# Turning a group's row maxima with VectorE's 32x32 transpose and eight small transfers instead of a TensorE transpose

## What is computed

```python
q = x @ q_w.T + q_b
xd = conv(x, stride 2) + conv_b
k = xd @ k_w.T + k_b
v = xd @ v_w.T + v_b
att = jnp.einsum('bhnd,bhmd->bhnm', q, k) * scale
att = jax.nn.softmax(att, axis=-1)
out = jnp.einsum('bhnm,bhmd->bhnd', att, v)
return out @ out_w.T + out_b
```

## Time and profile before

| | us |
|---|---|
| median of 3 runs | 3911.18 |
| lowest and highest run | 3905.49, 3913.1 |
| span of the profiled execution | 3912.8 |
| TensorE busy | 3836.0 (98%) |
| VectorE busy | 3334.3 (85%) |
| ScalarE busy | 2612.8 (67%) |

### The profile page before, as it was taken

The page is one execution under the profiler, slowest core; times in us unless marked ns, Lnnn a source line. Parts: engine busy times, 40 slices in busy tenths (PEclk is TensorE's granted clock), DMA queues, the critical chain, the costliest instruction groups (busy, mean ns, idle before and its releaser), DMA issues. The chain is left out here.

```text
span 3912.8 us, 76603 instructions
## 1 busy us (share of the span) xinstructions
PE 3836.0 (98%) x22744; PEld 1996.5 (51%) x22744; DVE 3334.3 (85%) x4142; ACT 2612.8 (67%) x4969; POOL 844.9 (22%) x553
## 2 busy tenths in 40 slices
PE   8979999999999999999999999999999999999998
PEld 5643333333333333333333333333334899999998
DVE  9979998999899899989989998999996777777775
ACT  4428887888788788878878887888887334343343
POOL 6522100000000000000000000000001787787775
PEclk9979999999999999999999999999999999999999
DMA  8991133115103311510231051024111222222220
GB/s 295 345 201 58 50 48 56 33 34 70 34 27 49 56 33 34 70 34 27 47 57 34 29 68 38 30 46 59 33 36 58 78 85 83 67 86 78 72 86 27
DMA packets 315388, 269.34 MB, mean 69 GB/s; under 512 B 156593, under 2 KB 225201, under 8 KB 315314
## 3 DMA queue, kind: packets, MB, share of 16 engines
q1 hardware_dynamic: 314194, 264.36, 27.6%
q0 software_dynamic: 1120, 4.19, 0.4%
HBM read 157.30 MB, written 110.10 MB: 68 GB/s over the span
## 5 line engine op out<-in xcount | busy, mean ns | idle before, releaser
L751 DVE TENSOR_REDUCE half_max<-first_ps 128x2 f32<-128x1024 f32 x2038 | 2402.0, 1221 | 280.1 <-PE first_ps L590 276.1
L717 ACT ACTIVATE probs<-score_ps 128x512 f32<-128x512 f32 x4096 | 2114.7, 603 | 578.4 <-PE score_ps L615 577.8
L615 PE MATMUL score_ps<-q_s,k_s 49*128 49x512 f32 x4096 | 1444.2, 477 | 23.5 <-DMA q_s<-max_row 12.8
L615 PEld LDWEIGHTS score_ps<-q_s,k_s 49*128 49x128 f32 x4096 | 574.6, 185 | 1284.4 <-ACT probs L717 1156.1
L625 PE MATMUL pv_ps<-probs,v_s 128*32 128x512 f32 x8192 | 1102.2, 610 | 0.0
L590 PE MATMUL first_ps<-k_s,q_s 48*128 48x512 f32 x4076 | 903.3, 421 | 14.2 <-PEq L189 9.5
L860 POOL TENSOR_TENSOR num<-num,rden 128x1024 f32<-128x1024 f32 x2 | 4.7, 2373 | 2585.3 <-DMA rden<-rden_d 2585.3
L1035 ACT ACTIVATE act_f<-fc_ps,b 128x512 f32<-128x512 f32 x256 | 174.9, 684 | 470.4 <-PE fc_ps L988 468.3
L590 PEld LDWEIGHTS first_ps<-k_s,q_s 48*128 48x128 f32 x4076 | 408.6, 188 | 61.5 <-issue 10.9
L1112 DVE CAST a_hi<-act_f 128x512 fp32r<-128x512 f32 x256 | 241.9, 946 | 146.6 <-ACT act_f L1035 146.0
L1164 POOL TENSOR_TENSOR a_lo<-act_f,a_hi 128x512 fp32r<-128x512 f32 x256 | 339.4, 1331 | 86.1 <-DVE a_hi L1112 86.1
(11 more groups left out here) (109 smaller groups left out, 2540.0 us busy)
## 6 DMA issues: line engine op xcount, KB each, us to landing
q_s<-q_hi_d SPq DMA_DIRECT2D x512, 64.0 KB, 2.1
o_d<-o_sb SPq DMA_DIRECT2D x128, 256.0 KB, 2.1
x_t<-x_c_in SPq DMA_DIRECT2D x32, 512.0 KB, 5.8
q_hi_d<-q_hi SPq DMA_DIRECT2D x32, 512.0 KB, 4.8
q_lo_d<-q_lo SPq DMA_DIRECT2D x32, 512.0 KB, 5.1
k_s<-k_hi_d SPq DMA_DIRECT2D x128, 128.0 KB, 4.3
q_s<-q_lo_d SPq DMA_DIRECT2D x256, 64.0 KB, 2.1
x_res<-x_in SPq DMA_DIRECT2D x32, 512.0 KB
```

Of the source, the lines that this page charges most:

```text
L615: pe.matmul(bank(s, u)[:, :], k_s[g][at, a, t * P:(t + 1) * P], q_s[g][at, a, :], start=True, stop=True).then_inc(scored, 1)
L717: nc.scalar.activation(probs[s % 2][:, u, :], bank(s, u)[:, :], ACT.Exp).then_inc(exped, 1)
L751: dve.reduce_max(half_max[g % 2][:, :, a * TT + t, keys], first_ps[keys][:, :, :], AX.X)\
```

## The change

The maxima are no longer turned by TensorE. `neg_max` becomes 128 x 32 (16 columns used, the others set to zero once) and VectorE transposes it in four 32x32 squares: in square k, the partitions 32k to 32k+15 then hold the 16 rows for the queries 32k to 32k+31. `max_row` therefore has the 16 rows in four pieces on four groups of partitions, and SP assembles the row of q_s with eight transfers in place of two: two halves of the heads x four squares, each from 8 partitions with 128 bytes of each. TensorE's `turn_max` and its two waits are gone, and so is the turn's slot in the ring of score banks; since 4 x 32 scores per block don't divide by 3, one bank is skipped at each block's first step, with the waits adapted. VectorE's `rows` keeps its place in the order and waits for `maxed` instead of `turned`.

```diff
-        neg_max = [sb(f"neg_max{i}", [P, TT * HG]) for i in two]
-        max_row = [sb(f"max_row{i}", [TT * HG, P], F32R) for i in two]
+        SQ = 32
+        neg_max = [sb(f"neg_max{i}", [P, SQ], F32R) for i in two]
+        max_row = [sb(f"max_row{i}", [P, SQ]) for i in two]
...
-        maxed, turned, row_up = (sem(n) for n in ("maxed", "max_turned", "row_up"))
+        maxed, blank, row_up = (sem(n) for n in ("maxed", "neg_max_blank", "row_up"))
...
-        QL, KVL, ML, OS = 6 * 16, 7 * 16, 2 * 16, 16
+        QL, KVL, ML, OS = 6 * 16, 7 * 16, 2 * (P // SQ) * 16, 16
...
-        AFTER = TURN + 2
+        SKIP = 1
 
         def bank(s, u):
 
-            return score_ps[(4 * s + u + (s - AFTER + KT) // KT) % RING]
-
-        assert (4 * STEPS + G) % RING == 0
+            return score_ps[(4 * s + u) % RING]
+
+        assert (4 * STEPS + SKIP) % RING == 0
...
                 for h in half_rows:
                     at = h * HALF + KROWS
                     row = q_s[g][at:at + 1, :, :].rearrange("p a (t q) -> p (a t) q", t=TT)
-                    sp.dma_start(row.bitcast(F32), max_row[g % 2][h * 2 * TT:(h + 1) * 2 * TT, :].bitcast(F32))\
-                        .then_inc(m_loaded[g], 16)
+                    for k in range(P // SQ):
+                        square = max_row[g % 2][k * SQ + h * 2 * TT:k * SQ + (h + 1) * 2 * TT, :]
+                        sp.dma_start(row[:, :, k * SQ:(k + 1) * SQ].bitcast(F32), square).then_inc(m_loaded[g], 16)
...
-            def turn_max(n, s):
-
-                g = (s - TURN) // KT + 1
-                pe.wait_ge(maxed, G * n + g + 1)
-                if s > 0:
-                    pe.wait_ge(exped, 4 * (STEPS * n + s + 1) + 2 + RING)
-                pe.transpose(bank(s + 1, 4)[0:TT * HG, 0:P], neg_max[g % 2][:, :], ident[:, :]).then_inc(turned, 1)
-
...
-                behind_turn = t == AFTER
-                if behind_turn and u == 2 and (more or s + KT - 2 < STEPS):
-                    pe.wait_ge(row_up, 1 + G * n + g + 2)
-                near = behind_turn and u < 2
-                pe.wait_ge(exped, 4 * (STEPS * n + s) + u + 1 + near)
+                skipped = SKIP if s == 0 and u < RING - SKIP else 0
+                pe.wait_ge(exped, 4 * (STEPS * n + s) + u + 1 + skipped)
...
-                    if s % KT == TURN and (more or s + KT < STEPS):
-                        turn_max(n, s)
...
-                if part - LEAD == TURN - KT:
-                    turn_max(0, part - LEAD)
...
-                    dve.tensor_reduce(neg_max[g % 2][:, :], halves, AX.X, ALU.max, negate=True)\
+                    dve.tensor_reduce(neg_max[g % 2][:, 0:TT * HG], halves, AX.X, ALU.max, negate=True)\
                         .then_inc(maxed, 1)
...
-                dve.wait_ge(turned, G * n + g + 1)
-                dve.tensor_copy(max_row[g % 2][:, :], bank(s + 1, 4)[0:TT * HG, 0:P]).then_inc(row_up, 1)
+                dve.wait_ge(maxed, G * n + g + 1)
+                dve.transpose(max_row[g % 2][:, :], neg_max[g % 2][:, :].bitcast(F32)).then_inc(row_up, 1)
...
+            for i in two:
+                dve.memset(neg_max[i][:, :].bitcast(F32), 0.0).then_inc(blank, 1)
+            dve.wait_ge(blank, 2)
```

## The result

| | us |
|---|---|
| before, median of 4 runs | 3911.24 |
| after, median of 4 runs | 4426.17 |
| ratio after to before, 95% interval | 1.1318 (1.1295 to 1.1342) |
| span of the profiled execution after | 4419.6 |

The change makes the kernel 13.2% slower, 515 us; the forecast was 611 us in a range of 239 to 829.

What follows compares the result with a forecast made beforehand. Bound by a TensorE-ScalarE loop of 2.60 us a step, TensorE busy 98%. 121 ordinary groups at 2.53 + 2.5 - 0.22 = 4.81 us (582) plus seven at 4.10 (29) add 611 us: 4522 us, range 4150 to 4740.

Steps and rivals of the forecast that it cites:

- The wait: TensorE at each group's first score: rows land 6.99 us after the first issue against 4.46, so it waits 2.53 us.
- the cover: Time from SP's first issue of the rows to the next group's first score: 4.69 us before, 4.46 after.
- The clock: TensorE after each wait: granted clock falls to 0.50, and slow steps lose 2.5 us more.
- six late cases: Groups of the kernel before whose first score waited on the row's transfer, 12.8 us in all; each had slow steps.
- The rival without clock loss: TensorE waits at each group's first score but its clock stays up: +309 us, 4220 us; chance 0.07.
- SP's refills: K and V loads on SP every fourth block: they hold SP long, but were forecast to add nothing.
- the seven turns of SP's outer loop: Groups whose rows are late already: only six further issues count, 4.32 - 0.22 = 4.10 us each, 29 us.
- The price of an issue: SP's max_row transfers: 0.65 us each, from the old line's row with the same eight rows; bounds 0.37 and 1.20.
- Short issue: Rival on SP's eight transfers: issues cost 0.37 us, rows land 0.57 us late, +45 us, 3956 us; chance 0.12.
- full gain: Rival: transfers land within 4.46 us and only TensorE's turn goes, 3911 - 28 = 3883 us; chance 0.05.

Runs made afterwards that it cites:

- The runs with two and with eight transfers: Changed kernel with two transfers in place of eight, maxima partly left out: 3890.18 us; kernel before, TensorE's turn kept, with eight transfers in place of two: 4436.17 us.
- the filled wait: Changed kernel with eight additional 512-column TensorE matmuls before the wait for the rows at each group's first score: 4260.17 us in one profiled run.
- the table: Kernel before with five additional SP transfers per group, of 16, 8, 4, 2 and 1 partitions of 128 bytes, timing each issue: 4007.11 us in one run.

## Why the prediction was right

**The mechanism** was right at each link: TensorE's transpose gone, the rows up at the same place in VectorE's order, eight issues in a row, the first score of each group waiting, slow steps behind it. The runs with two and with eight transfers show the first cause, the filled wait most of the second. The size was 96 us too high against the median, and 611 - 507 = 104 on the spans, in these terms:

| term | forecast us | measured us |
|---|---|---|
| VectorE's transpose | 0.19 | 0.20 |
| one issue | 0.65 | 0.635 |
| issue to next issue | 0.72 | (5.43 - 0.635) / 7 = 0.69 |
| last issue to the score | 1.95 | 6.60 - 7 x 0.69 = 1.77 |
| first issue to the score | 6.99 | 6.60 |
| wait of an ordinary group | 2.53 | 1.99 |
| slow steps behind a wait, mean | 2.5 | 243 / 121 new waits = 2.0 |

Of the 104 us, 44 are waits: the forecast holds 121 x 2.53 + 7 x 4.32 and the 12.8 that were there, 349 us, and 305 were measured. The other 60 are slow steps: 121 x 2.5 = 303 against 243.

**The wait.** I took the distance of issues from a pair, and the first two of the eight are indeed 0.72 us apart (median 0.717); from the third on it is 0.68. I took the landing from the 512-byte transfers of a late group; by the same reckoning the squares of 128 bytes landed 0.2 us sooner. Together that is 0.39 us. Another 0.15 was in the cover: 6.60 - 1.99 = 4.61 us against 4.46. The wait was thus 0.54 us, a fifth, too long.

**The clock.** I put the middle of six late cases behind every wait. The mean of the six is 2.6 as well, but their waits were 1.9 to 2.4 us; at 2.0 us 14 of 91 groups had no slow step. The rival without clock loss was wrong too.

**SP's refills: the step that failed.** I wrote that refilling K and V "holds SP for long, but its chain starts behind TensorE's own, later, step", and so cost it at nothing, the seven turns of SP's outer loop apart. The 34 waits of over 2.15 us, 121 us in all, are of four kinds. 14 of them, 44.8 us, lie in groups whose eight transfers stand behind a refill of K and V, as in the lines above: 16.8 us more than 14 ordinary waits. These are the cost that I had at nothing. Seven lie at the turns, also behind a refill, 32.4 us; I had 12.8 + 7 x 4.32 = 43 for those, too much. Ten, 23.0 us, are only 0.3 us above the ordinary ones. Three, 20.3 us, lie in the first two blocks, 14.3 us more than ordinary ones, and rotating SP's order leaves them (21.5 us). The refills and the start, some 31 us that I had at nothing, hid part of the terms that were too large. That the sum came so near was in part luck.

**The price of an issue** was taken from the right row, and the reason given for it, the eight rows, is not borne out: one to sixteen rows cost 0.547 to 0.675 us. The estimate held because the same line was measured, with the same eight rows and both ends in SBUF. The Trainium skill, "DMA: Bandwidth & Descriptors", section "Why a DMA increments its semaphore by 16 and not by 1", states that the issuing sequencer writes the increments of the engines that a transfer doesn't use. Read as a price, this would make four, two and one rows dearer than eight; the table shows 0.596, 0.587 and 0.547 against 0.675.

**Short issue and full gain.** With the measured cover and landing no group would have waited with issues under (4.61 - 1.77) / 7 = 0.41 us apart; they are 0.69. The full gain exists, 22 us with two transfers, but only where the transfers are hidden.

## What to carry to other kernels

Before an edit shortens a step on the engine that is busiest, look at what has its deadline at the end of that step: here the saved 0.22 us brought the deadline forward, and a transfer with no slack left took it back. Count issues on a queue, not only bytes: here seven times 0.69 us and the landing of the last, 6.60 us in all, were more than the 4.61 us that lay between the rows and their use, and the cure was to start earlier and to put the queue's patient work behind its urgent work. A wait on TensorE can cost more than its length when the clock falls behind it: here cutting the waits from 2.0 to 1.3 and to 0.63 us took 89 us from them each time, and 170 and 209 us from the kernel.

## What was not expected of the hardware

- Whether slow steps followed went steeply with the length of the wait: after 0 of 103 waits of 0.63 us, 54 of 96 of 1.3 us, 77 of 91 of 2.0 us.
- An issue of a transfer of 128 bytes per row from SBUF to SBUF cost 0.55 to 0.68 us whether it had one row or sixteen, and dearest were eight, 0.675.
- The bytes of these transfers didn't matter for their issue: in a burst the first took 0.667 us and the second 0.635 with 512 bytes a row, 0.664 and 0.640 with 128 (medians).
